# A fused attention and expert layer on one Trainium2 core: heads paired j with j+2, a new order of the attention work, and other placements of the last steps

## The chip, the cores and the metric

The kernel runs on one core of a Trainium2 chip. The core has four compute engines, TensorE (PE), VectorE (DVE), ScalarE (ACT) and GpSimd (POOL), a fifth, SyncE (SP), which here only issues DMAs, and 16 DMA engines. Each engine works through its own program in order and meets the others only at semaphores. The metric is the device time of one execution in microseconds (us), as the median of several runs. Matmuls are in fp32, except the scores, which are in fp32r.

## The reference

```python
def gnn(h, adj, Wq, bq, Wk, bk, Wv, bv, Wo, bo):        # h: (32, 256, 256), 8 heads of 32
    q, k, v = (split_heads(h @ W.T + b) for W, b in ((Wq, bq), (Wk, bk), (Wv, bv)))
    scores = einsum('bhqd,bhkd->bhqk', q, k) / sqrt(32)
    attn = softmax(where(adj == 0, -inf, scores), axis=-1)
    return merge_heads(einsum('bhqk,bhkd->bhqd', attn, v)) @ Wo.T + bo

def ffn(x, controller, f1, f2):                          # groups of t = 16 rows, 64 (expert, set) pairs
    logits = einsum('bgtd,des->bgtes', grouped, controller) + tie
    perm = (logits == max over t)                         # one row of each group for each pair
    inner = relu(einsum('bgtesf,bgtes->bgesf', einsum('bgtd,desf->bgtesf', grouped, f1), perm))
    return einsum('bgesd,bgtes->bgtd', einsum('bgesf,esfd->bgesd', inner, f2), perm)

x = x + gnn(layernorm(x), adj, ...)
x = x + ffn(layernorm(x), controller, f1, f2)
```

## The kernel before

**Attention** goes over 32 batches of 256 rows. A batch has two tiles of rows and four pairs of heads, so its scores are eight steps n = 2*pair + tile of two heads each. For a batch b each engine has these steps:

- PE: `h_transpose` (L459), `q_project` and `k_project` (both L466), `v_project` (L488), eight `scores` (L501, three PSUM banks in turn), eight `p_transpose` of the probabilities, one a head (L514, two banks in turn), `r_transpose` (L542), two `pv` of four heads (L528) and `o_project` (L551).
- DVE: `save_low` (L1024), which makes the low parts of k and q and thereby sets k_saved and q_saved; `maximum` (L1038), which adds the mask and takes the row maximum of a score step; `save_pt` for the even heads (L1049); `normalise` (L1063), `residual` (L1071), `sums_of_result`, `reciprocals`. In every second batch it also computes the statistics of two later batches (`sums_of`, `mean_variance`) and twelve short `norm_step`s. Such a batch is called "ahead" below.
- ACT: `apply_norm` (L802), `save_hT` (L794), `save_q` and `save_k` (L820), `exps` (L837), `save_pt` for the odd heads (L846), `save_v` (L810), `save_rbc` (L850).
- SP: `stack_parts` (L307), which copies the parts of q and k in SBUF into the stacks that the scores read: 16 DMAs of 128 KB a batch, four (r = 0 to 3) for each head j of a group of four. DMA (j, r) reads partitions 32j to 32j+31 and writes partitions 32r to 32r+31. The first eight of a batch release its first scores through one semaphore, the second eight its `scores(b, 2)` through another. For batch 0, ACT issues four of the first eight (L867).

The order is written out by hand in a function `batch` for each engine; in batch b the engines also do the projections of b+1, the normed rows of b+2, and the second half of the outputs of b-1. Batches 2 to 27 run in a loop, the others are unrolled. The PSUM bank `M[0]` serves h_transpose, k_project and v_project in turn, `M[1]` serves q_project, r_transpose and o_project.

**The expert layer** goes over four chunks of 16 tiles of 128 rows. A chunk has four units and then `experts`. A unit (PE: `unit_transpose` L559, `select` L663, `one_hot_transpose` L579, `logits` L572) sorts chosen rows into XS; POOL norms the rows of later units (L399). `experts` makes 16 products (`expand` L674, `contract` L695), and SP moves each (512 KB) to a DRAM scratch (L330). After all 16 have landed SP gathers them back as 16 tiles of 512 KB in another order (L340) into five slots; tile i from 5 on waits for the scatter of the pair of tiles (i-5)//2. PE `scatter` s (L722) takes the tiles 2s and 2s+1, DVE adds the result (`finish`, L1228), and SP stores it (L346). The scatters of chunk c-1 are placed in the units of chunk c by the function `scatters`: three in unit 1, three in unit 2, two in unit 3, the first after `one_hot_transpose`, the second after the third `select`, the third after the fourth `select`. `experts` waits for DVE's and ACT's copies of the selections of all units. The last chunk is gathered by four DMAs of 2 MB (L361) and scattered by eight `scatter_last` (L708), two for each DMA.

## Time and profile before

| | us |
|---|---|
| median of 3 runs | 801.06 (800.7 to 802.35) |
| profiled execution, its time | 803.15 |
| profiled execution, span from first to last instruction | 801.2 |
| start, to the first scores of the second batch | 0 to 41.55 |
| attention, the other 31 batches | 41.55 to about 538 |
| expert layer, four chunks | about 538 to 767 |
| gather, scatter and store of the last chunk | 767 to 801.2 |

The time outside the span is 803.15 - 801.2 = 1.95 us. PE is busy 91% of the span, DVE 76%, ACT 71%, POOL 16%. The mean granted clock of TensorE is 0.978 of full speed. The DMA engines are 50 to 70% busy in the attention and 80 to 100% in the expert layer. In a busy column an engine counts from the start of an instruction to its end; ends of matmuls are modelled and overlap the next start, so the starts are what to go by.

### The profile page before, as it was taken

The numbers are of one execution on the slowest core, as the hardware profiler recorded it, in microseconds if no ns is written. First come the engines' busy times: TensorE is split into PE (matmuls) and PEld (weight loads), VectorE is DVE, ScalarE is ACT, GpSimd is POOL, SyncE is SP. The second block draws the span as 40 slices with busy tenths as digits, with TensorE's granted clock in tenths as the row PEclk, the third lists the DMA queues.
The fourth block names the chain that finished last, engine by engine and source line by source line (L and its number), as shares of the span: only waits on it lengthen the run. The fifth ranks groups of instructions, "written<-read, shape, count | busy, mean of one in ns | idle before, by whom it ended". The sixth has DMA issues, their size and how long they took to land.

```text
span 801.2 us, 22540 instructions
## 1 busy us (share of the span) xinstructions
PE 729.8 (91%) x7296; PEld 561.2 (70%) x7296; DVE 612.3 (76%) x2558; ACT 567.7 (71%) x1654; POOL 125.4 (16%) x125
## 2 busy tenths in 40 slices
PE   7699999999999999999999999888998979986924
PEld 6588888888888888888888878665554555553601
DVE  3789898998998998988989988777556656655612
ACT  3698999999899899999999998755453443442500
POOL 1110001000100100010010004336325225200000
PEclk9999999999999999999999999999999999999967
DMA  5675576576666756765765665630589989889899
GB/s 157 156 181 139 133 169 146 130 170 154 146 147 153 171 131 146 170 155 121 170 153 131 139 150 137 196 121 2 216 317 323 348 293 337 340 310 338 355 309 305
DMA packets 102197, 157.60 MB, mean 197 GB/s; under 512 B 12288, under 2 KB 65024, under 8 KB 101888
## 3 DMA queue, kind: packets, MB, share of 16 engines
q1 hardware_dynamic: 99712, 155.04, 67.8%
q10 hardware_dynamic: 2432, 1.84, 1.0%
q8 instruction: 35, 0.57, 0.3%
q14 instruction: 18, 0.15, 0.1%
HBM read 47.78 MB, written 41.94 MB: 112 GB/s over the span
## 4 chain that ended last, share of the span: by engine, by line
PE 69%; DMA 14%; SPq 6%; DVE 6%; issue 3%; ACT 2%; DVEq 0%; ACTq 0%
PE bank L514 12%; PE bank L466 11%; DMA stage<-scratch 7%; PE bank L528 7%; PE bank L501 7%; PE bank L695 6%; PE bank L488 6%; PE bank L551 6%; SPq L307 5%; PE bank L674 5%; DMA XRlast<-scratch 2%; DMA stack<-parts 2%; PE bank L663 2%; DMA scratch<-stage 2%; PE bank L459 2%
## 5 line engine op out<-in xcount | busy, mean ns | idle before, releaser
L837 ACT ACTIVATE Ps<-Ps,nmax 128x256 f32<-128x256 f32 x512 | 255.3, 503 | 25.3 <-DVE nmax L1038 23.3
L1038 DVE CUSTOM_DVE_ANT_0 Ps<-bank,masks 128x256 f32<-128x256 f32 x512 | 198.9, 420 | 25.9 <-issue 24.0
L514 PE MATMUL bank<-ident,Ps 128*128 128x128 f32 x1024 | 145.8, 275 | 2.0 <-DVE PTs L1049 1.5
L514 PEld LDWEIGHTS bank<-ident,Ps 128*128 128x128 f32 x1024 | 116.2, 141 | 20.0 <-issue 11.9
L466 PE MATMUL bank<-hT,WT 128*128 128x256 f32 x512 | 122.1, 382 | 1.0 <-ACT hT L794 1.0
L501 PE MATMUL bank<-stack 128*128 128x256 f32 x512 | 118.1, 332 | 5.3 <-DMA stack<-parts 5.3
L387 POOL TENSOR_TENSOR X<-X,bob 128x512 f32 (+1 forms) x32 | 40.7, 1274 | 425.2 <-ACT hn L802 405.6
L466 PEld LDWEIGHTS bank<-hT,WT 128*128 128x128 f32 x512 | 93.4, 192 | 11.5 <-ACT WT L780 1.2
L399 POOL TENSOR_SCALAR h<-X,mv,roots 128x256 f32<-128x256 f32 x64 | 80.1, 1264 | 116.1 <-PE bank L663 87.4
L837 ACT ACTIVATION_READ_ACCUMULATOR Ps<-Ps,nmax 128x1 f32 x512 | 98.0, 191 | 0.0
L1049 DVE COPY PTs<-bank 128x512 f32<-128x512 f32 x128 | 87.7, 685 | 5.0 <-PE bank L514 4.8
L501 PEld LDWEIGHTS bank<-stack 128*128 128x128 f32 x512 | 80.5, 191 | 13.6 <-DMA stack<-parts 4.0
L246 ACT COPY XS<-bank 128x512 f32<-128x512 f32 x64 | 37.8, 590 | 60.1 <-PE bank L663 60.1
L846 ACT COPY PTs<-bank 128x512 f32<-128x512 f32 x128 | 73.8, 577 | 0.4 <-PE bank L514 0.4
L820 ACT ACTIVATE parts<-bank,few 128x256 fp32r<-128x256 f32 x128 | 53.7, 470 | 22.5 <-PE bank L466 20.8
L528 PE MATMUL bank<-PTs,Vs 128*32 128x256 f32 x1024 | 68.5, 385 | 0.0
L941 ACT COPY stage<-bank 128x512 f32<-128x512 f32 x64 | 37.5, 586 | 43.3 <-PE bank L695 43.3
L1270 DVE COPY stage<-bank 128x512 f32<-128x512 f32 x64 | 43.9, 691 | 27.6 <-PE bank L695 27.6
L246 DVE COPY XS<-bank 128x512 f32<-128x512 f32 x64 | 44.6, 696 | 25.9 <-PE bank L663 25.8
L488 PE MATMUL bank<-WT,hT 128*128 128x256 f32 x256 | 61.8, 384 | 1.8 <-DVE parts L1024 1.8
L1228 DVE TENSOR_TENSOR X<-X,bank 128x512 f32<-128x512 f32 x32 | 22.0, 688 | 54.2 <-PE bank L708 30.5
L551 PE MATMUL bank<-WT,OT 128*128 128x256 f32 x256 | 60.6, 379 | 1.4 <-DVE OT L1063 1.4
(86 smaller groups left out, 1037.0 us busy)
## 6 DMA issues: line engine op xcount, KB each, us to landing
stack<-parts SPq DMA_DIRECT2D x508, 128.0 KB, 2.4
scratch<-stage SPq DMA_DIRECT2D x64, 512.0 KB, 4.0
stage<-scratch SPq DMA_DIRECT2D x48, 512.0 KB, 6.2
X<-in_x SPq DMA_DIRECT2D x32, 256.0 KB, 2.8
out<-X SPq DMA_DIRECT2D x32, 256.0 KB, 4.8
XRlast<-scratch SPq DMA_DIRECT2D x4, 2048.0 KB, 17.1
f1s<-in_L_ffn_f SPq DMA_DIRECT2D x1, 2048.0 KB, 8.0
f2s<-in_L_ffn_f SPq DMA_DIRECT2D x1, 2048.0 KB, 14.1
```

Of the source, the lines that this page charges most:

```text
L246: return copy(XS[:, :, :, first:first + 4].rearrange("p k e (j two) -> p k e j two", two=2), banks[:, 4 + 2 * hf:6 + 2 * hf, 0:2 * P].rear ...
L399: last = nc.gpsimd.tensor_scalar(h2[n % NORMS][:, t, :], xtile(tile), mv2[:, tile, 0:1], roots[:, 1, tile:tile + 1], ALU.subtract, ALU.mult)
L466: last = nc.tensor.matmul(m[:, g * N:g * N + N], WT[:, w, k, g * P:g * P + P], hT[:, k, :], start=(k == 0), stop=(k == KT - 1))
L488: last = nc.tensor.matmul(M[0][:, t * D:t * D + D], hT[:, k, t * P:t * P + P], WT[:, 2, k, :], start=(k == 0), stop=(k == KT - 1))
L501: last = nc.tensor.matmul(s_bank(n)[:, h * N:h * N + N], stack[:, par, j, 0, g * N + t * P:g * N + t * P + P], stack[:, par, j, 1, g * N:g ...
L514: last = nc.tensor.transpose(PTb[h % 2][:, k * N + t * P:k * N + t * P + P], Ps[:, pr % 2, t, h % 2, k * P:k * P + P], ident[:, :])
L528: last = nc.tensor.matmul(Ob[32 * j:32 * j + 32, g * N:g * N + N], Vs[:, par, k, h * DH:h * DH + DH], PTs[:, h, k * N:k * N + N], start=(k ...
L551: last = nc.tensor.matmul(M[1][:, t * D:t * D + D], OT[:, g, t * P:t * P + P], WT[:, 3, g, :], start=(g == 0), stop=(g == G - 1))
L837: last = nc.scalar.activation(Ps[:, pr % 2, t, h, :], Ps[:, pr % 2, t, h, :], ACT.Exp, bias=nmax[:, pr % 2, t, h:h + 1], scale=-1.0, accum ...
L846: nc.scalar.copy(PTs[:, h, :], PTb[h % 2][:, :]).then_inc(pt_act, 1)
L1038: last = nc.vector.tensor_tensor_reduce(out=Ps[:, pr % 2, t, h, :], in0=s_bank(n)[:, h * N:h * N + N], in1=masks[:, t, :], scale=1.0, scal ...
L1049: nc.vector.tensor_copy(PTs[:, h, :], PTb[h % 2][:, :]).then_inc(pt_dve, 1)
```

## The change

1. **Pairs.** `head` and `slot_of` pair head j with head j+2 of a group of four. The first eight stack DMAs of a batch are those of j = 0 and 2, the second eight those of j = 1 and 3. In batch 0, ACT issues the four of j = 2.
2. **Start.** `h_transpose(1)` writes into the bank `Ob` ahead of `v_project(0)`, and `k_project(1)` runs ahead of the first scores. The wait for bo's bias moves behind them. ACT norms batch 1 ahead of `save_q(0)`; DVE does the statistics of batches 2 and 3 and five norm steps ahead of batch 0's `save_low`, and the other seven behind it.
3. **Order of a batch.** On PE both projections of k and q follow the first scores, the transposes of heads 6 and 7 of b-1 come behind `scores(b, 1)`, and scores are issued two by two. On DVE the two low parts of k come ahead of `maximum(1)` and those of q behind `maximum(2)`. The statistics of an ahead batch come ahead of `maximum(0)`, and its norm steps go into the second half. On ACT `save_k` and `save_q` come ahead of `exps(0)`. `h_transpose(b+2)` comes ahead of `pv(b, 0)`. In the last batch, its unit transposes, logits and `save_h2T` move likewise.
4. **Scatters.** Two in unit 1, three in unit 2, three in unit 3.
5. **End.** Eight DMAs of 1 MB instead of four of 2 MB, one for each `scatter_last`, and eight matmuls of 128 x 128 into the unused bank 5 behind each `scatter_last` but the last.

In the order of the file; the three `batch` functions (PE, ACT, DVE) stand with their context, of the rest only the changed lines do:

```diff
-last_in = [sem(f"last_in{i}") for i in range(4)]
+last_in = [sem(f"last_in{i}") for i in range(CT // 2)]
...
+def head(slot):
+    pr, half = divmod(slot, 2)
+    return pr // 2 * HPG + pr % 2 + 2 * half
+def slot_of(h):
+    g, j = divmod(h, HPG)
+    return 2 * (2 * g + j % 2) + j // 2
...
-    return ((), (0, 1, 2), (3, 4, 5), (6, 7))[u]
+    return ((), (0, 1), (2, 3, 4), (5, 6, 7))[u]
...
-        for j in range(HPG):
+        for j in (0, 2, 1, 3):
...
-                if not (isinstance(b, int) and b == 0 and j < 2 and r > 1):
-                    sp.dma_start(*stack_rows(par, j, r)).then_inc(stacked[par][j // 2], 16)
+                if not (isinstance(b, int) and b == 0 and j == 2):
+                    sp.dma_start(*stack_rows(par, j, r)).then_inc(stacked[par][j % 2], 16)
...
-    for i in range(4):
-        rows = slice((CHUNKS - 1) * CG + 4 * GPT * i, (CHUNKS - 1) * CG + 4 * GPT * (i + 1))
-        sp.dma_start(XRlast[:, 4 * i:4 * i + 4, :, :].rearrange("p t j d -> p (t j) d"),
+    for i in range(CT // 2):
+        rows = slice((CHUNKS - 1) * CG + 2 * GPT * i, (CHUNKS - 1) * CG + 2 * GPT * (i + 1))
+        sp.dma_start(XRlast[:, 2 * i:2 * i + 2, :, :].rearrange("p t j d -> p (t j) d"),
...
-    def h_transpose(b):
+    def h_transpose(b, into=M[0]):
...
-        if in_loop(b) or b > 0:
+        if in_loop(b) or b > 1:
...
-                last = nc.tensor.transpose(M[0][:, k * N + t * P:k * N + t * P + P],
+                last = nc.tensor.transpose(into[:, k * N + t * P:k * N + t * P + P],
...
-            g, j = divmod(2 * pr + h, HPG)
+            g, j = divmod(head(2 * pr + h), HPG)
...
-                                        Vs[:, par, k, h * DH:h * DH + DH], PTs[:, h, k * N:k * N + N],
+                                        Vs[:, par, k, h * DH:h * DH + DH], PTs[:, slot_of(h), k * N:k * N + N],
...
+    h_transpose(1, Ob)
     v_project(0)
     bias_product()
-    h_transpose(1)
-    pe.wait_ge(bias_done, 1)
+    pe.wait_ge(v_saved, 1)
+    k_project(1)
     def batch(b, par, last):
         first = isinstance(b, int) and b == 0
         late = isinstance(b, int) and b >= B - 2
         scores(b, par, 0)
+        if first:
+            pe.wait_ge(bias_done, 1)
+        if last:
+            pe.wait_ge(res_done, b - 1)
+            unit_transpose(0, (M[0], M[1]))
+        if not (first or last):
+            k_project(b + 1)
+        if not last:
+            q_project(b + 1)
+        scores(b, par, 1)
         if not first:
             p_transpose(prev(b), 6)
             p_transpose(prev(b), 7)
-        if last:
-            unit_transpose(0, (M[0], M[1]))
-        if not last:
-            k_project(b + 1)
-        scores(b, par, 1)
-        if not last:
-            q_project(b + 1)
         scores(b, par, 2)
+        scores(b, par, 3)
         if last:
             pe.wait_ge(ctl_in, 16)
             logits(0, M[0])
-        scores(b, par, 3)
         if not last:
             v_project(b + 1)
         scores(b, par, 4)
-        p_transpose(b, 0)
+        scores(b, par, 5)
         if not first:
             r_transpose(prev(b), last)
+        p_transpose(b, 0)
         p_transpose(b, 1)
         if not first:
             pv(prev(b), 1 - par, 1)
+        p_transpose(b, 2)
+        p_transpose(b, 3)
         if last:
             one_hot_transpose(0, M[0])
-        p_transpose(b, 2)
-        scores(b, par, 5)
-        p_transpose(b, 3)
         scores(b, par, 6)
         scores(b, par, 7)
         if not first:
             o_project(prev(b))
         p_transpose(b, 4)
-        p_transpose(b, 5)
+        if not late:
+            h_transpose(b + 2)
         if last:
             pe.wait_ge(perm_saved, 1)
             pe.wait_ge(res_done, b)
             unit_transpose(1, (M[0], M[1]))
         pv(b, par, 0)
-        if not late:
-            h_transpose(b + 2)
+        p_transpose(b, 5)
...
-        if s % 2 == 0:
-            pe.wait_ge(last_in[s // 2], 16)
+        pe.wait_ge(last_in[s], 16)
...
+        if s + 1 < CT // 2:
+            for _ in range(8):
+                nc.tensor.matmul(bank[5][:, 0:P], ident[:, :], ident[:, :], start=True, stop=True)
...
-    def save_hT(b):
+    def save_hT(b, src=M[0]):
...
-        nc.scalar.copy(hT[:, :, :], M[0][:, :]).then_inc(hT_saved, 1)
+        nc.scalar.copy(hT[:, :, :], src[:, :]).then_inc(hT_saved, 1)
...
-                                        accum_out=sums[:, 2 * pr + h, t:t + 1])
+                                        accum_out=sums[:, head(2 * pr + h), t:t + 1])
...
+    apply_norm(1, 1)
     save_q(0, 0)
     save_k(0, 0)
     act.wait_ge(q_saved, 1)
     act.wait_ge(k_saved, 1)
-    for j in range(2):
-        for r in (2, 3):
-            act.dma_start(*stack_rows(0, j, r)).then_inc(stacked[0][0], 16)
+    for r in range(4):
+        act.dma_start(*stack_rows(0, 2, r)).then_inc(stacked[0][0], 16)
     save_v(0, 0)
-    apply_norm(1, 1)
-    save_hT(1)
+    save_hT(1, Ob)
     def batch(b, par, last):
         first = isinstance(b, int) and b == 0
         late = isinstance(b, int) and b >= B - 2
         if not late:
             apply_norm(b + 2, par)
-        exps(b, 0)
-        if not last:
-            save_k(b + 1, 1 - par)
-        if not first:
-            save_pt(prev(b), 7)
         if last:
             save_h2T(0, (M[0], M[1]))
         if not last:
+            save_k(b + 1, 1 - par)
             save_q(b + 1, 1 - par)
+        exps(b, 0)
+        if not first:
+            save_pt(prev(b), 7)
         exps(b, 1)
         exps(b, 2)
-        exps(b, 3)
         if not first:
             save_rbc(prev(b))
+        exps(b, 3)
...
+        if not late:
+            save_hT(b + 2)
+        if last:
+            save_h2T(1, (M[0], M[1]))
         exps(b, 7)
         save_pt(b, 5)
-        if last:
-            save_h2T(1, (M[0], M[1]))
-        if not late:
-            save_hT(b + 2)
...
-    def reciprocals(b):
+    def reciprocals(b, between):
...
-        link(nc.vector.reciprocal(rsum[:, :, :], sums[:, :, :]))
+        mark(nc.vector.reciprocal(rsum[:, :, :], sums[:, :, :]))
+        between()
+        chain_wait()
...
-    def sums_of_result(b):
+    def sums_of_result(b, between=None):
...
+            if t == 0 and between is not None:
+                between()
...
+    sums_of(2)
+    mean_variance(mv, 2 * QT)
+    for i in range(5):
+        step(i, 2)
...
+    for i in range(5, ROOT_STEPS + 1):
+        step(i, 2)
...
-    sums_of(2)
-    mean_variance(mv, 2 * QT)
-    for i in range(ROOT_STEPS + 1):
-        step(i, 2)
...
-        maximum(b, 0)
         if ahead:
             sums_of(b + 3)
             mean_variance(mv, 2 * QT)
-        maximum(b, 1, lambda: norm_step(0))
+        maximum(b, 0)
         if not last:
             save_low(b + 1, 1 - par, 1, 0)
-            norm_step(1)
             save_low(b + 1, 1 - par, 1, 1)
+        maximum(b, 1)
+        maximum(b, 2)
+        if not last:
+            save_low(b + 1, 1 - par, 0, 0)
+            save_low(b + 1, 1 - par, 0, 1)
         if not first:
             save_pt(prev(b), 6)
-        norm_step(2)
-        maximum(b, 2, lambda: norm_step(3))
+        maximum(b, 3)
         if last:
             tied_logits(0, M[0])
-        norm_step(4)
-        if not last:
-            save_low(b + 1, 1 - par, 0, 0)
-            norm_step(5)
-            save_low(b + 1, 1 - par, 0, 1)
-        norm_step(6)
-        maximum(b, 3, lambda: norm_step(7))
-        norm_step(8)
+        save_pt(b, 0)
         if last:
             group_maximum()
-        save_pt(b, 0)
+        maximum(b, 4)
         if last:
             one_hot(0)
-        norm_step(9)
-        maximum(b, 4, lambda: norm_step(10))
-        norm_step(11)
         if not first:
             normalise(prev(b))
         maximum(b, 5)
-        maximum(b, 6)
+        norm_step(0)
+        maximum(b, 6, lambda: norm_step(1))
+        norm_step(2)
         save_pt(b, 2)
-        maximum(b, 7)
+        norm_step(3)
+        maximum(b, 7, lambda: norm_step(4))
+        norm_step(5)
         if not first:
             residual(prev(b))
+        norm_step(6)
         save_pt(b, 4)
+        norm_step(7)
         if not first:
-            sums_of_result(prev(b))
+            sums_of_result(prev(b), lambda: norm_step(8))
             mean_variance(mvr, QT)
+            norm_step(9)
             keep_statistics(prev(b))
-        reciprocals(b)
+        norm_step(10)
+        reciprocals(b, lambda: norm_step(11))
```

## Rows read from the trace of the kernel before

**Rows 1.** The page: busy time by engine, and the costliest group on ACT.
```profile
PE 729.8 (91%) x7296; PEld 561.2 (70%) x7296; DVE 612.3 (76%) x2558; ACT 567.7 (71%) x1654; POOL 125.4 (16%) x125
...
L837 ACT ACTIVATE Ps<-Ps,nmax 128x256 f32<-128x256 f32 x512 | 255.3, 503 | 25.3 <-DVE nmax L1038 23.3
```
**Rows 2.** Chain that ended last, at the start: start us, us, what.
```profile
21.51 4.74 DMA stack<-parts
...
27.15 2.88 PE bank L466 x8
```
**Rows 3.** Timeline at the start: start us, us, engine, line, operation, count, idle before.
```profile
16.20 0.88 DVE L1024 SCALAR_TENSOR_TENSOR parts<-bank,few,parts 128x256 fp32r<-128x256 f32 x2 [3.44 <-ACT parts L820]
...
21.95 0.59 ACT L810 COPY Vs<-bank 128x512 f32<-128x512 f32 x1 [4.06 <-issue]
...
30.10 1.89 PE L466 MATMUL bank<-hT,WT 128*128 128x256 f32 x8
...
41.55 0.48 PE L501 MATMUL bank<-stack 128*128 128x256 f32 x2
```
**Rows 4.** SP's stack DMAs (L307) issued from 18.8 to 23 us, issue to landing.
```profile
DMA to landing us min/median/max: 2.4/4.2/4.7
```
**Rows 5.** Windows: PE, PEld, DVE, ACT, POOL busy, PEclk, DMA share, GB/s.
```profile
22.00:26.00 4.00, 0.66 (x4) 0.42 (x4) 3.75 (x17) 2.11 (x4) 2.49 (x2) 0.99 0.95 208
26.00:30.00 4.00, 3.61 (x12) 3.12 (x13) 1.74 (x12) 2.08 (x6) 0.96 (x1) 0.58 0.78 181
...
228.00:259.26 31.26, 31.26 (x242) 26.26 (x241) 28.72 (x143) 28.57 (x91) 2.55 (x2) 1.00 0.64 151
```
**Rows 6.** Timeline of PE over one pair of batches in the loop.
```profile
238.65 1.07 PE L528 MATMUL bank<-PTs,Vs 128*32 128x256 f32 x16
...
243.18 1.04 PE L514 MATMUL bank<-ident,Ps 128*128 128x128 f32 x8
...
245.15 0.66 PE L459 MATMUL bank<-ident,hn 128*128 128x128 f32 x4
...
260.63 0.66 PE L459 MATMUL bank<-ident,hn 128*128 128x128 f32 x4
```
**Rows 7.** Timeline of DVE in the ahead batch of that pair.
```profile
240.06 0.69 DVE L1063 TENSOR_TENSOR OT<-bank,rbc 128x512 f32<-128x512 f32 x1
...
242.11 0.69 DVE L1049 COPY PTs<-bank 128x512 f32<-128x512 f32 x1
```
**Rows 8.** Timeline of SP in the same batch.
```profile
237.53 10.25 SPq L307 DMA_DIRECT2D stack<-parts  x16
```
**Rows 9.** Chain that ended last, batch 3 and batch 28.
```profile
65.44 1.90 SPq L307
...
466.02 3.75 DMA stack<-parts
```
**Rows 10.** Timeline of PE, units of the third chunk.
```profile
662.63 0.73 PE L663 MATMUL bank<-permR,h 32*128 32x128 f32 x16
...
664.78 0.64 PE L722 MATMUL bank<-stage,permT 128*32 128x256 f32 x8 [0.63 <-DMA stage<-scratch]
...
667.03 0.66 PE L579 MATMUL bank<-ident,permT 128*128 128x128 f32 x4
...
680.64 1.07 PE L722 MATMUL bank<-stage,permT 128*32 128x256 f32 x16
...
683.45 0.75 PE L674 MATMUL bank<-XS,f1s 128*32 128x128 f32 x20 [1.08 <-DVE XS L246]
```
**Rows 11.** Timeline: PE's 128 x 128 matmuls at the start; the last scatters and DVE's last add.
```profile
9.14 0.61 PE L435 MATMUL bank<-ident 128*128 128x128 f32 x4
...
788.75 1.93 PE L708 MATMUL bank<-XRlast,permT 128*32 128x256 f32 x32 [2.39 <-DMA XRlast<-scratch]
...
794.69 3.22 PE L708 MATMUL bank<-XRlast,permT 128*32 128x256 f32 x32 [4.00 <-DMA XRlast<-scratch]
...
797.99 0.69 DVE L1228 TENSOR_TENSOR X<-X,bank 128x512 f32<-128x512 f32 x1 [0.61 <-PE bank L708]
```

## Prediction

> **What bounds the kernel now.** I read the page's busy times first [rows 1], then the windows, the chain in order of time, and the timelines of each stage, since PE's 91% is a mean over four stages with different limits. In the attention loop a pair of batches takes from one window edge to the next 31.26 us, and PE has work in all of it, at full clock, while DVE has 28.72 and ACT 28.57 [rows 5]. The two batches of the pair are not equal: the plain one takes 260.63 - 245.15 = 15.48 us, so the ahead one takes 15.78 [rows 5, 6]. The start is bound by the first stack transfers, then by projections at a low clock [rows 2]. In the expert layer, the gathered tiles arrive last: the last scatter of a chunk starts as its tile lands, and the experts start 2.8 us after it [rows 10]. The end is a chain of last DMA, two scatters, one add and one store [rows 11].
>
> **Start.** Before, the first scores follow the last of eight landings at 21.51 + 4.74 = 26.25, the k projection of batch 1 then takes 2.88 us and q's starts at 30.10 [rows 2, 3]. PE had 0.66 us of work between 22 and 26, and the granted clock then fell from 0.99 to a mean of 0.58, so to its lower level of 1.2 GHz for most of the next 4 us [rows 5]. After, k_project(1) waits for V's and hT's copies: ACT starts V's at 21.95, two copies of 0.59 end at 23.1 [rows 3], and 1.7 us of projection (q's at full clock took 1.89 with its tail [rows 3]) end at 24.8, inside the wait for the stack. PE is then busy just ahead of 26, so I take the full clock afterwards. The q projection starts at 26.65, is read at 28.7 and saved at 29.5. ACT then has six steps of exps of 2 x 0.503 [rows 1] and two copies of some 0.5 up to what transposes 4 and 5 need: 29.5 + 6.0 + 1.0 = 36.5. PE's transposes, h_transpose and pv behind them cost 2.4 (from 243.18 to 245.15 in the loop is 1.97 for two transposes and pv [rows 6], and h_transpose's 0.4). So batch 1's scores start at 38.9 instead of 41.55 [rows 3]: **2.7 us gained**. The bounds are 0 (a late transfer for batch 1) and 4.1. The latter holds if the stack lands before 24.8, and then k_project ends last. The moved work is free: ACT's norming of batch 1 lies in PE's projection, and DVE's statistics of batch 2 go into 3.44 us of idle time ahead of save_low [rows 3]. They need about 1.4 + 0.4 + 5 x 0.2 = 2.8 us; if x came late, they would delay save_low one to one.
> On the transfers: four are issued by each queue as before, and the landing grew from 2.4 to 4.7 us when both queues issued [rows 4]. So both queues share a limit, and this is why I keep 26.25. A sentence by itself: the Trainium skill, page "SBUF — State Buffer", section "Door 1: The DMA port swizzle", says that partitions 0 to 63 reach only the 8 even ports and 64 to 127 the 8 odd ones. By it, heads 0 and 1 read one half of the ports and heads 0 and 2 read both, and the whole change would give 789.1 (a rival below). But the page "DMA: Bandwidth & Descriptors", section "Rules for kernel authors", speaks against it: two transfers to disjoint halves of the partitions share the same 16 engines and serialize, which leaves 790.6. No row before has two such sources at once. Both queues now also write the same r at the same time, where before they wrote different halves.
>
> **The loop.** PE's work is the same, instruction for instruction. What an order can change is the cost at each change of kind. I compared starts: two scores between projections cost as much as between transposes, within 0.1 us, so I take 15.4 to 15.5 us for PE alone in either order. The 0.3 us of an ahead batch is DVE's: its statistics and steps delay maximum(1), the low parts of k and so v_project. After, the statistics fall in a hole (DVE waits for k's high part anyway) and v_project waits no more: -0.3 in 13 batches. But a new wait comes up in every batch. In the new order pt4 (the transpose of head 4) needs DVE's copy of head 2, which is queued behind normalise, maximum(5) and maximum(6). From pv's start a: normalise starts at a + 1.41 (240.06 against 238.65) and the copy at a + 3.46, which is the same distance as before (242.11) [rows 6, 7]; it is complete at a + 4.2. Before, PE needed it at 243.18 = a + 4.53 [rows 6]. After, two scores fewer lie between pv and pt4, so PE is there at about a + 4.13. It waits 0.07 us in a plain batch and, with three norm steps of some 0.08 ahead of the copy, 0.3 in an ahead batch. Behind pt4 wait h_transpose, pv and the next scores, so this counts in full. Sum for the pair: -0.3 + 0.3 + 0.07 - (0 to 0.1) = 0. **I take 0 for the loop**, with 0.25 us a pair to either side, so ±3 us. DVE's own load, 28.72 of 31.26 [rows 5], leaves it room, and ACT's order leaves exps(3) 0.3 us ahead of pt2.
> **Stack waits.** SP issues 16 DMAs in 10.25 us [rows 8]. The last one lands 2.4 us later, which left 0.6 to 1.0 us to `scores(b, 2)`. An issue of 1.90 instead of 0.6 cost PE about 0.9 in batch 3 and 0.4 in batch 4; landings of about 3.75 instead of 2.4 cost 0.7, 0.7 and 0.5 in batches 28 to 30 [rows 9]. After, q_saved comes at 7.1 us after a batch's first scores in both kinds of batch (before 7.1 and 7.7), and `scores(b, 2)` 0.1 later, so the margin is about 1.05. **1.7 us gained** of the 3.2, bounds 0 and 3.2. In the last batch the second stack half still lands 4.2 us after its first scores and PE has little to do before it; exps(7) now waits for the second save_h2T. I take 0.2, bounds -1 and +1.
>
> **Scatters.** The last scatter of the third chunk starts at 680.64, and the experts start at 683.45: 1.0 us of scatter, then a select of 0.66 and the copies of it [rows 10]. After, the select and its copies are done ahead of the last scatter: 1.8 us less in each of three chunks (1.5 in the last). Against it, scatter 2 moves from 664.4 to behind the next unit's transpose, select and one_hot_transpose, so it ends near 662.63 + 0.66 + 2.27 + 1.0 = 666.6 instead of 665.35, 1.2 us later [rows 10], and the gathers of tiles 9 and 10, which wait for it, are issued 1.2 later. About 3.5 us of earlier transfers are still in flight then, so I let 0.6 of the 1.2 reach the last tile in two chunks. In the last chunk the units have no transposes and scatter 2 waits for its tile in both orders, so nothing. 3 x 1.8 - 0.3 - 2 x 0.6 = 3.9: **4.0 us gained**, bounds 1.5 and 5.3. The maximum over regions and the adds on DVE follow the same order and lie beside it.
>
> **End.** Before, two scatters at the lower clock and the wait for them lie between the last landing (794.6) and the last add (797.99): 3.35 us. Two scatters at full clock took 1.93 [rows 11]. After, one scatter is behind the last landing. At full clock the add starts about 1.15 after it, so 2.2 less, at half clock 2.0 after it, so 1.35 less. The 8 matmuls of 128 x 128 take 4 x 0.43 = 1.75 at full clock (two in a run of four records of 0.61, tail included [rows 11]) and fit into the 3.3 us between two landings with a scatter of 1.0. The last stores share the ring, which may hold back 0.4. **1.7 us**, bounds 0.5 and 2.3. It costs nothing unless the matmuls are still running when the last tile lands.
>
> **Rivals.**
> - **The read side is the limit of the first stack.** Then it lands before 24.8 and 1.4 us more is gained: 789.1. For it: all eight sources were partitions 0 to 63. Against it: both queues now write the same r together.
> - **The loop gets faster.** The new wait at pt4 is hidden and 0.3 us a pair stays: 13 x 0.3 = 4, so 786.6. For it: the 0.07 is smaller than my error.
> - **The scatters return nothing** since the gather ends later by what is saved: 790.6 + 4.0 = 794.6. For it: the DMA engines are near their limit there.
> - **DVE's copy of head 2 comes later than I think** and PE waits 0.4 us more in each of 30 batches: 790.6 + 12 = 802.6, and at 0.45 it is 804. It decides from 0.35 us a batch, above which the change is slower than before. For it: the ahead batch packs statistics, eleven steps and eight maxima into DVE, and the copy has no slack left. Against it: DVE has 2.5 us free in a pair. Half of that price gives 797.
>
> **How the numbers follow.** Gains: 2.7 + 0 + 1.7 + 0.2 + 4.0 + 1.7 = 10.3. The profiled execution would go from 803.15 to 792.8. It stood 2.1 above the median of 801.06, which gives 790.8; I say **790.6**. Chances: forecast 0.42, first stack 0.20, faster loop 0.12, scatters 0.12, half the DVE delay 0.05, all of it 0.06, no change 0.03. Measurement can tell about 0.2% (1.6 us) from no change. Faster 0.90, same 0.04, slower 0.06. The range 784.5 to 797 takes in all but the last cases and sums of two small misses.
>
> **What would show it.** Batch 1's first scores near 38.9; pairs of 31.2 ± 0.25 us with idle time of PE at L514 released by DVE's L1049; no wait above 0.5 us for the stack in batches 3, 4 and 28 to 30; experts starting within 1.3 us of the last scatter's start; a clock of 1.0 in the last 10 us and a last add some 1.2 us after the last landing. A loop pair above 31.9 us would make the prediction wrong, as would a gather that ends over 1.5 us later in each chunk.

## The result, and the profile after

The changed kernel takes 791.36 us (median of 4 executions, 788.79 to 795.41) against 801.46 us for the kernel before on the same chip: a ratio of 0.988, 95% interval 0.9842 to 0.9919. That is 10.1 us less, by the interval 6.5 to 12.7. The prediction was 790.6 in a range of 784.5 to 797. The time was forecast well; the sum behind it was not, and this section and the next ones show where the terms went.

The profiled execution of the changed kernel was the slowest of its four (795.41 us, span 793.2). Page, busy time and the two groups that matter below:

```profile
span 793.2 us, 22744 instructions
PE 737.7 (93%) x7408; PEld 572.9 (72%) x7408; DVE 608.9 (77%) x2558; ACT 564.6 (71%) x1654; POOL 125.4 (16%) x125
...
L511 PE MATMUL bank<-stack 128*128 128x256 f32 x512 | 107.3, 321 | 5.1 <-DMA stack<-parts 5.1
...
XRlast<-scratch SPq DMA_DIRECT2D x8, 1024.0 KB, 12.1
```

PE's busy time is 7.9 us longer [rows 1]; the matmuls added between the last scatters take 15.8 of it, so the rest has become shorter by as much as the span. The line numbers moved: scores are L511 (before L501), projections L476, transposes of P L524, pv L538, the scatters L735 and L721, the first expert matmuls L688.

**Start.** Timeline of PE in the changed kernel: start us, us, engine, line, operation, count, idle time before and what ended it.

```profile
22.93 1.96 PE L476 MATMUL bank<-hT,WT 128*128 128x256 f32 x8 [1.38 <-ACT hT L810]
27.22 0.51 PE L511 MATMUL bank<-stack 128*128 128x256 f32 x2 [2.32 <-DMA stack<-parts]
27.56 1.89 PE L476 MATMUL bank<-hT,WT 128*128 128x256 f32 x8
...
30.81 0.74 PE L511 MATMUL bank<-stack 128*128 128x256 f32 x4 [1.13 <-DMA stack<-parts]
...
38.27 0.66 PE L524 MATMUL bank<-ident,Ps 128*128 128x128 f32 x4 [1.66 <-ACT Ps L853]
...
40.70 0.48 PE L511 MATMUL bank<-stack 128*128 128x256 f32 x2
```

The k projection of batch 1 did move into the wait for the stack (22.93, full clock). But the first scores start at 27.22, not at 26.3, and then `scores(0, 2)` waits for the **second** half of the stack until 30.81. Batch 1's first scores start at 40.70; before it was 41.55 [rows 3]. So 0.85 us are gained where 2.7 were forecast.

**Loop.** Windows of the changed kernel (PE, PEld, DVE, ACT, POOL busy, PEclk, DMA share, GB/s); the third is one pair of batches. Below it PE's and then DVE's timeline in the plain batch of that pair.

```profile
22.00:26.00 4.00, 1.96 (x8) 1.44 (x8) 0.28 (x1) 2.62 (x6) 3.64 (x3) 1.00 1.07 217
26.00:30.00 4.00, 2.47 (x12) 2.05 (x12) 1.83 (x9) 0.51 (x2) 0.08 (x1) 1.00 0.90 192
297.95:328.94 30.99, 30.99 (x242) 26.12 (x241) 28.50 (x143) 28.37 (x91) 2.55 (x2) 1.00 0.65 152
```

```profile
313.46 1.07 PE L538 MATMUL bank<-PTs,Vs 128*32 128x256 f32 x16
...
315.86 1.89 PE L561 MATMUL bank<-WT,OT 128*128 128x256 f32 x8
317.59 0.60 PE L524 MATMUL bank<-ident,Ps 128*128 128x128 f32 x4
...
328.94 1.07 PE L538 MATMUL bank<-PTs,Vs 128*32 128x256 f32 x16
```

```profile
314.59 0.69 DVE L1079 TENSOR_TENSOR OT<-bank,rbc 128x512 f32<-128x512 f32 x1
...
316.60 0.69 DVE L1063 COPY PTs<-bank 128x512 f32<-128x512 f32 x1
```

A pair takes 30.99 us, 0.27 less than before [rows 5]; its batches take 15.51 and 15.48. Head 4's transposes start 4.13 us after pv (317.59 - 313.46), which is where the prediction put PE, and no wait stands before them. DVE's copy of head 2 starts at pv + 3.14 and is done by pv + 3.8 in this plain batch; the prediction had 3.46 and 4.2.

**Chunks and end.** The experts now start 0.46 us after the last scatter's second half, which waits for its tile; before they started 2.8 us after the start of the last scatter, which waited for the same tile [rows 10]. But tiles wait longer for their slots. Timeline of PE at the end of the second gather of the changed kernel, and PE and DVE in the last 7 us:

```profile
673.78 0.64 PE L735 MATMUL bank<-stage,permT 128*32 128x256 f32 x8 [0.54 <-DMA stage<-scratch]
674.24 0.95 PE L688 MATMUL bank<-XS,f1s 128*32 128x128 f32 x28
```

```profile
786.57 2.05 PE L781 MATMUL bank<-ident 128*128 128x128 f32 x16
786.70 0.69 DVE L1248 TENSOR_TENSOR X<-X,bank 128x512 f32<-128x512 f32 x1 [2.29 <-PE bank L721]
788.55 1.07 PE L721 MATMUL bank<-XRlast,permT 128*32 128x256 f32 x16
789.69 0.69 DVE L1248 TENSOR_TENSOR X<-X,bank 128x512 f32<-128x512 f32 x1 [2.29 <-PE bank L721]
```

The last tile had landed at 787.46, and PE was still busy with the eight extra matmuls (L781) until 788.55. It was late by a microsecond from the second scatter on: the first scatter and its eight matmuls ran mostly at the low clock and took 5.2 us, and from there on eight matmuls and a scatter take 2.98 us, hardly less than the 3.0 us between two tiles, so the delay stays. Window of that first group (clock 0.53):

```profile
765.40:770.60 5.20, 5.20 (x32) 3.86 (x32) 0.69 (x1) 0.00 (x0) 0.00 (x0) 0.53 1.09 353
```

Where the time went, between the two profiled executions: to the first select of the expert layer 537.82 before and 532.53 after (5.3 us gained); the three chunks from first select to the fourth experts 202.9 and 200.7 (2.2 gained); from there to the end 60.6 and 60.0 (0.6). That is 8.1 of a span that went from 801.2 to 793.2.

### The profile page after: what moved, and what is told of

It is laid out like the page before. It is cut to its first block, busy times and chain, and to the rows that moved or that the text cites. A ratio compares the mean times of both kernels' runs of the same rounds, so it can differ in the third digit from the quotient of the medians.

```text
span 793.2 us, 22744 instructions
## 1 busy us (share of the span) xinstructions
PE 737.7 (93%) x7408; PEld 572.9 (72%) x7408; DVE 608.9 (77%) x2558; ACT 564.6 (71%) x1654; POOL 125.4 (16%) x125
## 4 chain that ended last, share of the span: by engine, by line
PE 81%; DMA 10%; DVE 3%; SPq 2%; ACT 2%; issue 1%; DVEq 0%; ACTq 0%
PE bank L524 14%; PE bank L476 14%; PE bank L538 8%; PE bank L511 7%; PE bank L561 7%; PE bank L498 7%; PE bank L709 6%; DMA stage<-scratch 6%; PE bank L688 5%; PE bank L677 3%; SPq L317 2%; PE bank L735 2%; DMA scratch<-stage 2%; PE bank L781 2%; PE bank L552 2%; PE bank L469 2%
## 5 line engine op out<-in xcount | busy, mean ns | idle before, releaser
L1052 DVE CUSTOM_DVE_ANT_0 Ps<-bank,masks 128x256 f32<-128x256 f32 x512 | 196.0, 420 | 8.7 <-issue 7.0
L524 PE MATMUL bank<-ident,Ps 128*128 128x128 f32 x1024 | 142.1, 277 | 2.7 <-ACT Ps L853 2.2
L524 PEld LDWEIGHTS bank<-ident,Ps 128*128 128x128 f32 x1024 | 113.2, 141 | 34.6 <-issue 24.7
L476 PE MATMUL bank<-hT,WT 128*128 128x256 f32 x512 | 116.1, 379 | 2.3 <-ACT hT L810 2.3
L511 PE MATMUL bank<-stack 128*128 128x256 f32 x512 | 107.3, 321 | 5.1 <-DMA stack<-parts 5.1
L397 POOL TENSOR_TENSOR X<-X,bob 128x512 f32 (+1 forms) x32 | 40.7, 1273 | 421.4 <-ACT hn L818 402.0
L476 PEld LDWEIGHTS bank<-hT,WT 128*128 128x128 f32 x512 | 94.8, 190 | 14.5 <-ACT Vs L826 1.8
L511 PEld LDWEIGHTS bank<-stack 128*128 128x128 f32 x512 | 76.3, 191 | 10.1 <-DMA stack<-parts 6.0
L538 PE MATMUL bank<-PTs,Vs 128*32 128x256 f32 x1024 | 68.5, 385 | 0.0
L1038 DVE SCALAR_TENSOR_TENSOR parts<-bank,few,parts 128x256 fp32r<-128x256 f32 x128 | 55.9, 478 | 11.4 <-ACT parts L836 11.4
L498 PE MATMUL bank<-WT,hT 128*128 128x256 f32 x256 | 60.6, 379 | 1.4 <-DVE parts L1038 1.4
```

Source lines behind the costliest of these rows:

```text
L476: last = nc.tensor.matmul(m[:, g * N:g * N + N], WT[:, w, k, g * P:g * P + P], hT[:, k, :], start=(k == 0), stop=(k == KT - 1))
L498: last = nc.tensor.matmul(M[0][:, t * D:t * D + D], hT[:, k, t * P:t * P + P], WT[:, 2, k, :], start=(k == 0), stop=(k == KT - 1))
L511: last = nc.tensor.matmul(s_bank(n)[:, h * N:h * N + N], stack[:, par, j, 0, g * N + t * P:g * N + t * P + P], stack[:, par, j, 1, g * N:g ...
L524: last = nc.tensor.transpose(PTb[h % 2][:, k * N + t * P:k * N + t * P + P], Ps[:, pr % 2, t, h % 2, k * P:k * P + P], ident[:, :])
L538: last = nc.tensor.matmul(Ob[32 * j:32 * j + 32, g * N:g * N + N], Vs[:, par, k, h * DH:h * DH + DH], PTs[:, slot_of(h), k * N:k * N + N], ...
L1038: low = nc.vector.scalar_tensor_tensor(parts[:, par, 2 * which + 1, g, :], M[1 - which][:, g * N:g * N + N], (bqs, bks)[which][:, g:g + 1] ...
```

## The experiments

All are compared with the kernel before on the same chip by the ratio of the times. One ratio carries an interval of 0.2 to 0.5% to either side, so effects of 1 us are read from the traces, and the ratios serve to see that nothing large is hidden.

**The changed kernel again** (no edit).

> The changed kernel itself once more, beside the kernels below on the same chip, with more rounds than the first result (four executions, 788.8 to 795.4 us). If the first result stands, the ratio to the kernel before is 0.988 and the median near 791.2. Its trace is a second sample of the parts that differ from one execution to the next (gathers, stack waits of batch 3, half-clock stretches): the attention loop should come out as before to 0.01 us a batch, 15.48 and 15.51, the chunks anywhere from 55 to 60 us.

792.24 us, ratio 0.9892 (0.9857 to 0.9928). Batches of 15.48 and 15.51 us to 0.01 again; the chunks 57.0, 56.0 and 56.5 where the first trace had 56.4, 58.1 and 59.0. So the attention loop is fixed by the program, and the gathers differ by some us from one execution to the next. A single pair of traces can't give the scatters' worth.

**The order alone**: the kernel before with the new bodies of the attention batch for PE, ACT and DVE.

```
 scores(b, par, 0)
-p_transpose(prev(b), 6), p_transpose(prev(b), 7)
 k_project(b + 1)
-scores(b, par, 1)
 q_project(b + 1)
+scores(b, par, 1), p_transpose(prev(b), 6), p_transpose(prev(b), 7)
 ...
```

(These are PE's first steps; the rest of its order, ACT's and DVE's go with it.)

> The kernel before with the new order of the attention batches alone, on PE, ACT and DVE (heads in pairs j and j+1, the first transfers, the start, the scatters and the end stay as before). By the prediction's terms the loop gives 0, the stack waits 1.7 and the last batch 0.2, so about 1.9 us in all: 799.5. By what the trace of the changed kernel shows (pairs of 30.99 instead of 31.27 us, 13 of them, 3.6 us; stack waits gone, about 2.5; last batch about 1.2 longer) it is about 4.9: 796.5. If the loop's gain came from the pairing of the heads instead, the pairs stay at 31.27 and the time at 800 or above. A wait at the transpose of head 4 would show in every batch by the prediction (0.07 and 0.3 us), and not at all by the rival of the faster loop.

Batches of 15.48 and 15.51: the whole gain of the loop, with heads j and j+1 still together. The waits for the stack in batches 28 to 30 are gone too. The first select comes at 532.46, 5.4 us earlier than before. No wait before head 4's transposes. The rival "the loop gets faster" holds in the trace, and the order alone makes it. The median is 798.44 us, ratio 0.998 (0.9955 to 1.0004), a gain of 1.6 with up to 3.6 us inside the interval. That is less than the 5.4 us of the traces. The kernel before has one trace only, of an execution 2.3 us slower than the median beside it (800.85), while the execution traced here was 1.9 us faster than its own. Part of the 5.4 are stack waits, which vary. The loop's 3.6 us repeat in all 13 pairs of each trace, but they lie at the edge of the interval, so the times don't confirm them, and why the whole gained less stays open.

**Where in the order the loop's gain lies.** Two kernels put DVE's work back and keep PE's and ACT's new order. First the statistics alone:

```
+maximum(b, 0)
 if ahead: sums_of(b + 3); mean_variance(mv, 2 * QT)
-maximum(b, 0)
```

> The changed kernel with DVE's statistics of batch b+3 (four sums, a mean and variance, 1.9 us) back behind the first maximum of the batch, ahead of the low parts of k. If the gain of the loop comes from having taken them out of the way of k's low part and v's projection, as the prediction's term of 0.3 us says, an ahead batch goes from 15.51 back to about 15.75 us and a pair to 31.25, with a wait of PE for the third scores or v's projection. If the gain lies in the new order of PE's blocks, the pair stays at 30.99.

A pair stayed at 30.99 us (791.88 us, ratio 0.9877, 0.9823 to 0.9931). Then also the twelve norm steps, to their old places between the low parts and the first five maxima:

> The changed kernel with DVE's statistics of batch b+3 and the twelve norm steps back among the first five maxima of a batch, between and behind the low parts of k and q, as in the kernel before. The orders of PE and ACT and all else stay new. With the statistics alone moved back a pair stayed at 30.99 us. If the 0.28 us a pair come from where the norm steps stand, an ahead batch goes from 15.51 to about 15.8 and a pair to 31.27, about 3.6 us in the whole: 795. If they come from PE's new order, in which k's and q's projections stand together and give DVE time for the low part of k, the pair stays at 30.99 to 31.05 and the time at 791 to 792.

Windows of this kernel over one pair:

```profile
298.86:329.82 30.96, 30.96 (x241) 26.15 (x240) 28.38 (x143) 28.42 (x91) 2.54 (x2) 1.00 0.65 153
```

30.96 us: not slower, but 0.03 faster, with both batches at 15.48 (793.44 us, ratio 0.9891, 0.9836 to 0.9946). So the loop's gain doesn't come from where DVE's statistics and steps stand. It comes from what this kernel keeps of the new order: PE's, ACT's, and on DVE the low parts of k ahead of `maximum(1)` and the copy of head 6 behind those of q. Which of these does it wasn't tested apart.

Where the ahead batch lost its 0.3 us can be read from PE's timeline in the kernel before, first in an ahead batch, then in a plain one:

```profile
234.47 0.82 PE L501 MATMUL bank<-stack 128*128 128x256 f32 x4
236.82 0.59 PE L501 MATMUL bank<-stack 128*128 128x256 f32 x2
...
240.06 0.49 PE L501 MATMUL bank<-stack 128*128 128x256 f32 x2
240.88 0.73 PE L501 MATMUL bank<-stack 128*128 128x256 f32 x4
...
250.26 0.82 PE L501 MATMUL bank<-stack 128*128 128x256 f32 x4
252.46 0.59 PE L501 MATMUL bank<-stack 128*128 128x256 f32 x2
...
255.70 0.49 PE L501 MATMUL bank<-stack 128*128 128x256 f32 x2
256.38 0.72 PE L501 MATMUL bank<-stack 128*128 128x256 f32 x4
```

Around v's projection the ahead batch takes 2.35 us and the plain one 2.20, since DVE's low part of k comes late. Around the transposes of head 3 it is 0.82 against 0.68, since they wait for ACT's copy of head 1. So half of the 0.3 us was v's projection and half a copy on ACT. In the new order k's and q's projections stand together, 3.3 us of PE work, and scores go two by two ahead of the transposes; that this is what lets DVE and ACT catch up fits both, but is argued.

**How much room DVE has.** One instruction more ahead of the copy of head 2, in each batch but the last:

```
 norm_step(2)
+if not last: nc.vector.memset(LT[:, :], 0.0)
 save_pt(b, 2)
```

> The changed kernel with one more DVE instruction in each batch, a memset of 128 x 256 that nothing needs, some 0.3 us long, directly ahead of the copy of head 2 (the step of which the prediction said that the transposes of head 4 wait for it). In the trace of the changed kernel that copy is complete about 0.3 us ahead of the transposes in a plain batch and 0.1 us in an ahead batch. By that, 0.3 more give back 0 to 0.1 in the plain and 0.2 to 0.3 in the ahead batch: pairs of 31.2 to 31.4 instead of 30.99 us, with idle time of PE ahead of the transposes. If PE is bound by itself with room to spare, nothing moves; if DVE were the bound, a pair would take 0.6 more.

The windows of one pair, the added instruction, and pv's starts on PE's timeline:

```profile
302.26:333.49 31.23, 31.21 (x241) 26.05 (x240) 28.82 (x145) 28.39 (x91) 2.54 (x2) 1.00 0.63 151
```

```profile
305.70 0.27 DVE L1207 MEMSET LT<- 128x256 f32 x1
```

```profile
302.26 1.07 PE L538 MATMUL bank<-PTs,Vs 128*32 128x256 f32 x16
...
317.98 1.07 PE L538 MATMUL bank<-PTs,Vs 128*32 128x256 f32 x16
...
333.49 1.07 PE L538 MATMUL bank<-PTs,Vs 128*32 128x256 f32 x16
```

0.27 us of DVE work per batch cost 0.21 us in the ahead batch (15.72 instead of 15.51) and 0.03 in the plain one (15.51 instead of 15.48): 31.23 a pair, 795.77 us, ratio 0.9932 (0.9912 to 0.9953), where the changed kernel has 0.988 to 0.9892. The mechanism of the prediction's slow rival is there: the copy of head 2 is next behind PE. By these numbers its distance was 0.06 us in the ahead batch and 0.24 in the plain one.

**The pairs**: heads j and j+1 together again.

```
-return pr // 2 * HPG + pr % 2 + 2 * half
+return slot
-for j in (0, 2, 1, 3):
+for j in range(HPG):
-act.dma_start(*stack_rows(0, 2, r))
+act.dma_start(*stack_rows(0, 1, r))
 ...
```

> The changed kernel with heads j and j+1 in one step again: the stack is sent in the order 0, 1, 2, 3, SyncE sends head 0's four first transfers and ScalarE head 1's four. By the prediction the pairing is worth nothing: 791.4, with the first scores at 27.2 us as in the changed kernel. By the rival of the read side, eight sources in partitions 0 to 63 land later than four in 0 to 31 and four in 64 to 95: the first scores come 1 us or more later, the stack waits of batches 2 to 4 and 28 to 30 come back in part, and the time is 793 or above.

The eighth transfer lands at 26.41 us, 5.2 us after the first; in the changed kernel the eighth of all transfers lands at 26.61, 5.1 us after its first. That is one landing in 0.74 and in 0.73 us, the first with both sources in partitions 0 to 63 (heads 0 and 1), the second with one in 0 to 31 and one in 64 to 95 (heads 0 and 2). Over all traces it is 0.71 to 0.74 with heads 0 and 1 and 0.70 to 0.76 with heads 0 and 2. The rival of the read side, which needed the stack before 24.8 us, falls: both pairings pass a transfer of 128 KB in about 0.7 us. The time, 794.78 us, ratio 0.992 (0.989 to 0.9951), is 0.3 to 0.4% above the changed kernel with intervals that overlap. Its trace shows 1.4 us of it as a stack wait in batch 3, which other kernels here have too or not (below). Whether the pairing is worth something beyond this stays open.

**The start**: k's projection of batch 1 behind the first scores again.

```
-h_transpose(1, Ob)
 v_project(0); bias_product()
-pe.wait_ge(v_saved, 1); k_project(1)
+h_transpose(1, Ob)
+pe.wait_ge(bias_done, 1)
 ...
-if not (first or last): k_project(b + 1)
+if not last: k_project(b + 1)
```

> The changed kernel with k's projection of batch 1 behind the first scores again (the first transfers on two queues, the pairs and the orders stay). By the prediction's working, which lets the first stack half and then the projections set batch 1's start, it costs 2.7 us: batch 1's first scores at 43.4 instead of 40.7. By the trace, in which scores 2 of batch 0 waits for the second stack half until 30.8 us in the changed kernel and until 32.0 before, the projection lies inside that wait in both places: 0 to 0.9 us, first scores of batch 1 at 40.7 to 41.6.

Timeline of PE in this kernel:

```profile
26.96 0.77 PE L511 MATMUL bank<-stack 128*128 128x256 f32 x2 [4.90 <-DMA stack<-parts]
27.52 4.77 PE L476 MATMUL bank<-hT,WT 128*128 128x256 f32 x16
31.95 1.06 PE L511 MATMUL bank<-stack 128*128 128x256 f32 x6
...
42.63 0.48 PE L511 MATMUL bank<-stack 128*128 128x256 f32 x2
```

Batch 1's first scores start at 42.63, 1.9 us later than in the changed kernel: between the two expectations. The two projections behind the first scores take 4.4 us, partly at the low clock, and end at 31.95, 0.6 us after the second stack half has landed (31.34). So between these two traces moving k is worth 1.9 us. But the eight traces that have k moved and the rest of the start unchanged reach batch 1 at 40.46 to 42.61, on the mean at 41.13; by the mean it is 1.5, and two single traces don't fix it. Against the kernel before only 0.85 is left (0.4 on the mean), and the other parts of the change take the difference. With the changed transfers the first scores come 0.1 to 0.8 us later than the 26.39 of before; and the kernel with the order alone, whose first scores start at 26.04, reaches batch 1 at 41.90. A likely reason is that the new order puts both copies of batch 1's projections ahead of the first exps. The time, 792.89 us (0.9891, 0.9865 to 0.9917), is too coarse for this.

**The scatters**, first with the old spread:

```
-return ((), (0, 1), (2, 3, 4), (5, 6, 7))[u]
+return ((), (0, 1, 2), (3, 4, 5), (6, 7))[u]
```

> The changed kernel with the scatters of three chunks spread as before, (0, 1, 2), (3, 4, 5) and (6, 7) over units 1 to 3. By the prediction 4.0 us come back: 795.4. By the traces of the two kernels, in which the three stretches from one chunk's first expand to the next were 3.1 and 0.8 us shorter and 1.7 us longer, it is 2.2: 793.6. By the rival that the gathers end later by what is saved, nothing: 791.4.

794.14 us, ratio 0.9926 (0.9902 to 0.9951), 0.34 to 0.46% above the changed kernel. Then a mixed one, with three scatters in unit 1 as before and the last select ahead of the last scatters as after:

```
-return ((), (0, 1), (2, 3, 4), (5, 6, 7))[u]
+return ((), (0, 1, 2), (3, 4), (5, 6, 7))[u]
```

> The changed kernel with the scatters of a chunk as (0, 1, 2), (3, 4) and (5, 6, 7) over units 1 to 3: three behind the last select as in the changed kernel, three in unit 1 as before. In nine gathers with the old spread the last tile landed 28.2 us after the first was issued and the experts started 2.4 to 3.1 (once 4.0) us behind it; in nine with the new one the tile landed at 30.0 and the experts started 0.5 us behind it. If the later landing comes from scatter 2, which is moved from unit 1 to unit 2 and holds back the gathers of tiles 9 and 10, it goes here: landing at about 28.5 and experts at 0.5, periods near 56 us, 3 to 4 us faster than the changed kernel. If it comes from scatter 5, which holds back tile 15, or from the DMA engines, it stays at 30.0: no change.

791.1 us, ratio 0.9875 (0.9853 to 0.9898). The traces of all kernels say more than these two times, since each has one of three spreads. From the landings that they record, in us (means; in brackets the lowest and highest sum):

```
spread   traces  first gather issued   last landing to   three periods,
                 to last landing       experts           sum
old      3       28.2                  2.9               174.1 (172.3 to 175.7)
new      9       29.8                  0.6               171.7 (169.5 to 173.5)
mixed    2       28.6                  0.6               169.2 (169.0 and 169.4)
```

The new spread takes 2.3 us from each tail and gives 1.6 back to each gather on the mean (1.2, 1.4 and 2.3 in the first, second and third): 2.3 us for three chunks. The ranges of the old and the new spread overlap, and the mixed one rests on two traces. The tail shows in the group of L688, first of the kernel with the old spread, then of the changed one:

```profile
L688 PE MATMUL bank<-XS,f1s 128*32 128x128 f32 x1024 | 41.3, 283 | 3.8 <-DVE XS L256 3.8
```

```profile
L688 PE MATMUL bank<-XS,f1s 128*32 128x128 f32 x1024 | 40.3, 278 | 0.8 <-DVE XS L256 0.8
```

PE's wait for DVE's selected copies ahead of the experts falls from 3.8 to 0.8 us. SyncE's total wait for scatters that free a slot doesn't tell the new spread from the mixed one (43.8 to 46.5 us with the old, 47.3 to 50.9 with the new, 47.8 twice with the mixed one). The single tiles do, in us from the first gather's issue (means over 9, 27 and 6 gathers):

```
spread   tile 9 issued   tile 9 landed   tile 15 issued   tile 15 landed
old      13.4            19.0            22.8             28.2
new      15.2            19.8            24.2             29.8
mixed    13.4            18.9            23.8             28.6
```

Tile 9 waits for scatter 2. With the new spread it is issued 1.8 us later, and the tiles behind it fall back; with scatter 2 in unit 1 again it is issued and lands as before, and the last tile is only 0.4 us late. So most of the later landing (1.2 of 1.6 us) came from scatter 2. The 0.4 fit scatter 5, which still moves to unit 3 and on which tile 15 waits.

**The matmuls between the last scatters**, none, four and (in the last kernel) six instead of eight:

> The changed kernel without the eight matmuls of 128 x 128 between two scatters of the last chunk. By the prediction they keep the clock, and without them the last scatter and the wait for it cost 2.0 instead of 1.15 us: 0.85 us slower, 792.2. By the trace of the changed kernel they are themselves the pace: eight of them and a scatter take 2.98 us at full clock, the tiles land every 3.0 us, and the last scatter started 1.1 us after its tile had landed. Then without them the last scatter starts at once and takes 0.9 us more at the lower clock: no change within 0.3 us.

> The changed kernel with four instead of eight matmuls of 128 x 128 between two scatters of the last chunk. In the runs with eight, and in the run with none, 5.7 us lie between the last landing and the end: with eight the last scatter starts 1.1 us late at full clock, with none it starts at once and takes 1.98 instead of 1.04 us at the lower clock. Four take about 1.0 us and leave PE free before the next tile. If half of the work still holds the clock, the last scatter starts at the landing at full clock and the distance is 4.7 us: about 1 us faster, 790.4. If the clock falls as with none, 5.7 us and no change. The prediction held that the eight cost nothing.

790.71 us (0.9874, 0.9838 to 0.991) and 791.95 us (0.989, 0.9869 to 0.9911). Timeline of the last scatter and add without them:

```profile
784.00 1.93 PE L721 MATMUL bank<-XRlast,permT 128*32 128x256 f32 x16 [1.01 <-DMA XRlast<-scratch]
786.00 0.69 DVE L1245 TENSOR_TENSOR X<-X,bank 128x512 f32<-128x512 f32 x1 [2.25 <-PE bank L721]
```

From the last landing to the end it is 5.74 us with eight, 5.71 with none, 5.77 with four. With none the scatter starts at the landing and takes 1.93 at the low clock; with eight it takes 1.07 and starts 1.1 late. (In the nine traces with eight it starts 0.6 to 1.2 us late, and the end is at 5.74 or 5.75 in each.) With four the clock is held and the scatter starts at the landing:

```profile
783.96 1.07 PE L721 MATMUL bank<-XRlast,permT 128*32 128x256 f32 x16 [0.78 <-DMA XRlast<-scratch]
```

The add follows at 785.10, 1 us earlier against its tile than in the other two. Still the end stays where it was: the last store takes 3.46 us from issue to landing, against 2.38 with eight and 2.53 with none. In all twelve traces with eight last transfers it lands 5.3 to 5.4 us after the last gather, whether it is issued 1.9 or 3.1 us after it. The trace records the landing of a DMA in 16 steps, and these tell why. With four matmuls, all but four of the 32 steps of the last two stores come by 4.3 us after the last gather, two at 4.7, and the last two at 5.3 and 5.4. Window of the last of that work (4.3 to 5.0 us after the landing):

```profile
788.20:788.90 0.70, 0.00 (x0) 0.00 (x0) 0.00 (x0) 0.00 (x0) 0.00 (x0) 0.75 0.13 47
```

A DMA share of 0.13 is two of 16 engines: two lag behind the others, and the store isn't complete before they are done. With eight matmuls (the first trace of the changed kernel), 14 steps of the last store come at 4.9 to 5.1 and the last two at 5.3 as well. The lag is there already in the gather: of its last transfer 14 or 15 steps come 0.9 to 2.1 us ahead of the last one. So while they lag, an earlier add doesn't bring the end forward. What holds these engines back stays open.

**A combination**: the mixed spread, six matmuls, and for batch 0 alone exps(0) ahead of q's copy on ACT and q's low part ahead of the third maximum on DVE.

> The changed kernel with three edits: scatters as (0, 1, 2), (3, 4) and (5, 6, 7); six instead of eight matmuls between the last scatters; and in batch 0 ScalarE's first exps ahead of its copy of q, and DVE's low part of q ahead of the third maximum. The last two lie in the chain to batch 1's first scores: q's low part waited for a maximum that waits for the second stack half (32.05 us). Expected: batch 1's first scores at 39.9 to 40.2 instead of 40.7 us; chunk periods of 56.3 instead of 57.3 us on average (3 us); six matmuls take 1.5 and a scatter 1.0 us of the 3.0 between two tiles, and if that holds the clock, the end comes 4.7 us behind the last landing instead of 5.7, otherwise no change. Together 3 to 5 us below the changed kernel, 787 to 788. If the time between executions is set by the gathers' own spread, the difference is below 1 us.

790.11 us, ratio 0.9857 (0.9825 to 0.9889), beside 792.24 for the changed kernel on the same chip: 2.1 us faster by the medians, with intervals that overlap. The chunks keep their part (sum 169.4). The other two edits give nothing in its trace, each for a reason that a row shows, and the stack wait of batch 3 costs 1.8 us in it. The start, on PE's timeline and in its window:

```profile
27.14 3.22 PE L476 MATMUL bank<-hT,WT 128*128 128x256 f32 x8
...
41.13 0.49 PE L511 MATMUL bank<-stack 128*128 128x256 f32 x2
```

```profile
26.00:30.00 4.00, 3.20 (x11) 2.67 (x11) 1.56 (x7) 1.09 (x4) 0.00 (x0) 0.69 0.85 184
```

The granted clock was 0.69 on average from 26 to 30 us, so q's projection ran mostly at the lower level and batch 1's first scores came at 41.13, the mean of the other kernels. What the new order of batch 0 is worth at full clock stays open. And the end:

```profile
783.77 1.07 PE L721 MATMUL bank<-XRlast,permT 128*32 128x256 f32 x16 [0.43 <-DMA XRlast<-scratch]
784.91 0.69 DVE L1255 TENSOR_TENSOR X<-X,bank 128x512 f32<-128x512 f32 x1 [2.34 <-PE bank L721]
```

Six do what four did: the scatter starts at the landing, the last add 1.2 us after it instead of 2.2, the last store takes 3.44 us, and the end is again 5.75 us after the landing. All but four steps of the last two stores come by 4.0 us after the last gather, and the last two again at 5.2 and 5.3.

## Why the prediction came out right, and which of its steps did not

The sum was 10.3 us. What the traces give for each term, once from the two profiled executions and once as the mean over the traces that share the part (eight with the changed start, order and transfers; nine with the changed spread; twelve with eight last transfers), always against the one trace of before, and for the chunks of the mean against the three with the old spread. That trace is of an execution 2 us slower than its kernel's median, so the sums can be too high by as much:

```
term              forecast   the profiled pair   mean
start             2.7         0.85                0.4
loop              0           3.6                 3.6
stack waits       1.7         2.1                 1.9
last batch        0.2        -1.2                 0.2
scatters          4.0         2.2                 2.3
end               1.7         0.6                 0.5
sum              10.3         8.1                 8.9
```

In the profiled execution the last batch lost 1.2 us, at a lower clock; its window:

```profile
508.00:514.00 6.00, 4.31 (x22) 2.98 (x21) 3.87 (x23) 3.81 (x14) 0.74 (x2) 0.74 0.94 322
```

The granted clock was 0.74 there. The other seven traces gain 0.4 to 0.5 us in the last batch. The start differs more, from 1.1 us gained to 1.1 lost, the latter with v's projection at the low clock.

The total came out right because the loop's 3.6 us, which the forecast held at 0 and gave a chance of 0.12, stood in for what the start, the scatters and the end did not bring (2.3, 1.7 and 1.2 us of the means). That errors of this size nearly cancel is luck. By its own signs the prediction failed in several places: batch 1's scores at 40.7 and not 38.9, the last add 2.2 and not 1.2 us after the last landing, no idle time at the transposes of head 4, and gathers that end 1.6 us later on the mean, where it had named 1.5 in each as proof against it.

- **Start: a wait left out.** The step that failed is the chain after 26.25. It went from the first stack half to q's projection and ACT's exps and never asked when the second half lands. The sixteen transfers of 128 KB land one every 0.60 to 0.69 us, whoever issues them, so the second half lands at about 30.8 (before: 31.6), and the third scores, their maxima and exps wait for it. ACT's exps began here:

```profile
30.22 0.51 ACT L853 ACTIVATE Ps<-Ps,nmax 128x256 f32<-128x256 f32 x1
```

  From there to head 4's transposes (38.27) it is 8.05 us; the forecast had 7.0, from 29.5 to 36.5. So of the 1.8 us that are missing 1.05 are such waits, and 0.7 the later start of the chain. Two other steps failed with it. The first half landed at 27.17 and not at 26.25 (26.4 to 27.0 in the other kernels with the changed start): SyncE goes on with the second half as soon as it has issued its four, and one of those transfers (landed at 26.61) overtook ScalarE's fourth. And "the full clock afterwards" held in some executions only; in the combination PE was idle for 2.25 us ahead of its first scores and q's projection ran at the low clock, after 2.32 idle us in the changed kernel it ran at full clock. The rival of the read side fell. The Trainium skill, page "DMA: Bandwidth & Descriptors", section "Rules for kernel authors", says that transfers to disjoint halves of the partitions share the same engines and serialize; the traces agree, with 0.7 us a transfer of the first half for either pairing.
- **Loop: two terms that were set against each other.** The -0.3 of the ahead batch was right in size, though v's projection was only half of it. The +0.3 and +0.07 for the new wait at head 4's transposes were not: PE is there at pv + 4.13 as forecast, but the copy is done at pv + 3.8 in the plain batch, and in the ahead batch just in time. The copy's distance (3.46 us) was taken from an ahead batch of the old order, where DVE, busy with norm steps, came to normalise only at pv + 1.41. In the new order it is there at pv + 1.1 in both kinds of batch; the copy follows at 3.14 in the plain batch, and at 3.36 with three steps ahead of it. The added memset shows that the margin is real and thin. And the reason given for the -0.3, the statistics moved into a hole, was wrong: with statistics and steps put back the loop is no slower. The rest of the new order does it.
- **Stack waits: right in kind.** In the trace of before all of them together cost 2.5 us, not 3.2. Those of batches 28 to 30 are gone in all traces with the new order, as a margin of 1 us instead of 0.6 lets expect. Those of batch 3 come and go: 0 to 1.8 us in the traces, 0.5 before. Chain of the kernel with the mixed spread, and what follows from it on PE:

```profile
64.83 2.26 SPq L317
```

```profile
78.54 0.73 PE L511 MATMUL bank<-stack 128*128 128x256 f32 x4 [1.25 <-DMA stack<-parts]
```

  One issue of 2.26 us instead of 0.6, at a time when SyncE issues without a pause, costs batch 3 1.5 us. Over the traces the wait follows this issue: nothing without it or with 1.4 us, 0.3 to 0.8 with 1.5 to 2.0, 1.3 to 1.8 with 2.1 to 2.3.
- **Scatters: tail right, gather mis-sized.** The tail lost 2.3 us (forecast 1.8) in each chunk. The gather's delay was taken as 0.6 in two chunks and nothing in the third, and was 1.2, 1.4 and 2.3. Two steps failed. Tiles 9 and 10 are issued 1.8 us later and not 1.2, and the "3.5 us of earlier transfers" still in flight covered a third of it and not half. And "scatter 2 waits for its tile in both orders" did not hold in the third: there tile 9 is issued 1.9 us later, and its gather is the longest on the mean (30.2 us). (The term's own sum gives 3.9, not 4.0.)
- **End: the wrong end of the chain.** The forecast had the eight matmuls done in 2.75 of 3.3 us with the scatter; they take 2.98 of 3.0, and they were still running when the last tile landed. But that is not what decided: with four or six PE is free in time and the end doesn't move. The step that failed is the one from the last add to the last store, which the forecast kept at its length but for 0.4 us. Before, the store took 2.13 us from its issue; now it is complete 5.3 us after the last gather, whenever it is issued. So the distance from that landing to the end fell from 6.6 to 5.74 us, 0.9 instead of 1.35 to 2.2. The eight transfers in place of four also end 0.3 us later (27.8 instead of 27.5 us after the last chunk's last write landed).
- **No wait at head 4, slow rival.** Given 0.11 in its two sizes; it did not occur, but 0.27 us of DVE work more in a batch brings it into every second batch.
